# The output matrix's transposing jobs, two at a time between pieces of the first batch's key and query products

## The chip, the cores and the metric
One core of a Trainium2 chip runs the whole program. The metric is the device time in microseconds from start to end; three runs of the kernel before gave 2906.24, 2908.05 and 2908.42 us. TensorE multiplies and turns tiles into PSUM, VectorE, ScalarE and GpSimd work on them, and SyncE issues the transfers. Each engine takes its own list of instructions in order and waits on counting semaphores for the others.

## What is computed
The reference is a small tower over 64 batches of 128 rows and 1024 columns:

```python
h = _L0_tok_ref(log_dt, x, B, inv_A_real, A_imag, 1024)   # state-space kernel over 1024 steps
h = h + _L0_attn_ref(_layernorm(h), wq, wk, wv, wo)       # 32 heads, 8 for keys and values, rotation, causal softmax
h = h + _L0_ffn_ref(_layernorm(h), W_base, b_base, lora_A, lora_B, router_W, router_b, prior, active)
```

The attention's mask leaves every causal position in for 128 rows. The last step is a dense layer with four low-rank experts, mixed by a router.

## The kernel before
A first stage (`token_kernel`, to about 215 us) makes the rows `h` and stores them. A second (`tower`) goes through the batches, one turn for each: a turn for `b` does attention for batch `b`, the key, value and query products for `n = b + 1`, the first norm for `m = b + 2`, the output product for `b - 1` and the dense layer for `b - 2`. The turns for `b = -2` and `b = -1` have only the parts that exist: the norm of batch 0, then the products of batch 0 and the norm of batch 1. Every engine has its own version of `turn`, and the order of work is what is written there, with counting semaphores between the engines.

All products are in 16 bit with split operands: a weight is kept as a high and a low half, so a dense product is, for each of eight pieces of 128 rows of the weight, three matmuls of 512 columns (`dense`). `kv(c0, c1)` does pieces c0 to c1 of the key and value product into a bank, `q(0, ...)` and `q(1, ...)` those of the two halves of the query product; each of the three has 24 matmuls.

The weights come as 32 bit and have to be turned and divided. That is a list of 56 jobs (`jobs`): 0 to 23 for query, key and value (`J_O` = 24), 24 to 39 for the output matrix (`J_B` = 40), 40 to 55 for the base matrix of the dense layer; `MID` is 30. A job is three steps on three engines: TensorE turns a part into a PSUM bank (`turn`; 4 transposes, for the output matrix 16 matmuls by the identity, on 32 columns each), ScalarE writes the high half from the bank (`high`), VectorE the low half (`low`), which counts `s_wlo`. The banks go round: a job waits until the low half of the job that had its bank before is done (`before`). `spread(i)` is one small matmul that gives the maximum over all partitions of a matrix to every partition; from it come the scales (`powers`).

What stands around the change, in the order of each engine:

- TensorE: jobs 10 to 29, `spread(4)`, then the turn for `b = -1`: `kv`, `q(0)`, `q(1)`, and `pe_close` with jobs 30 to 39. The turn for `b = 0` begins with the first score product, which waits for low half 38 (and the second for 39), then `spread(2)`, two jobs of the base matrix, and the key product of batch 1.
- ScalarE: `act_after` does the high halves of jobs 14 to 29, then waits for scale 4 and copies `lbs` (the low-rank experts' matrix). Then comes the turn for `b = -1`: sums of absolute values of the base matrix's eight parts (`base_sums`, for its scale), the 16-bit copies of the rotated heads (`heads_high`: k, 0, 1, 2, 3), the value half, the two instructions of the norm, and the high halves 30 to 39, at places that `act_early` gives by a name (`0`, `2`, `"norm"`, `"last"`).
- VectorE: `after` does the low halves 10 to 23, the maximum of `lbs` and its column for `spread(4)`, the low halves 24 to 29, the scale from `spread(4)`, and the low part of `lbs`. Then the turn for `b = -1`: the rotations of keys and queries (`rope`), the low parts of the heads, the statistics of the norm, and the low halves 30 to 39 by `early`.
- GpSimd adds the two parts of a rotation, and does the two small operations and the low half of the norm.
- SyncE issues the transposing transfers of heads and of normed rows, each behind the low part that it needs.

`after` and `act_after` stand ahead of the turn for `b = -1` on their engines. PSUM banks 2 and 3 hold `lbs` until its low part is done; job 32 waits for that.

Of the kernel before, what the change touches and what calls it, by code (L numbers as in the profile page):

```python
# [28 lines left out]
NQ, NO = NQKV // P, D // P  # L29
# [564 lines left out]
def prepare_weights(nc, sem, w, keep, ring, ps_b, ps_ar):  # L594
# [80 lines left out]
    class Prep:  # L675
        wlo, wt, lbs, bias, ps = s_wlo, s_wt, s_lbs, s_bias, s_ps
        ar_made, ar_copied, base_row = s_ar, s_arraw, s_rows[2]
        done_a, done_c, done_score, done_pv, done_half = last_a + 1, last_c + 1, (last[0] + 1, last[1] + 1), last[4] + 1, last[3] + 1
        jb, jend, mid = J_B, J_END, MID

# [71 lines left out]
        @staticmethod  # L752
        def act_early(act, b, k, unused):
            def base_sums(i0, i1):
                for i in range(i0, i1):
                    act.wait_ge(s_wb[GROUP[i]], 16 * GROUP.count(GROUP[i]))
                    if i:
                        act.wait_ge(s_sums, i)
                    nc.scalar.activation(unused, raw_a[:, NQ - NO + i], ACT.Abs,
                                         accum_out=part_max[:, i:i + 1]).then_inc(s_sums, 1)  # L760

            if b == -1 and k == 0:
                base_sums(0, 4)
            if b == -1 and k == 2:
                base_sums(4, 6)
            if b == -1 and k == "norm":
                Prep.high(act, MID, MID + 4)
                base_sums(6, NO)
            if b == -1 and k == "last":
                Prep.high(act, MID + 4, J_B)  # L770
            if b == 0 and k != "norm" and k != "last":
                Prep.high(act, J_B + 2 * k, J_B + 2 * k + 2)

        @staticmethod
        def dve_tools(dve):
# [97 lines left out]

            def early(b, k):
                if b == -1 and k == "last":
                    low(MID, MID + 4)
                    dve.wait_ge(s_sums, NO)
                    V.tensor_reduce(mx[:, 2:3], part_max[:, 0:NO], AX_X, ALU.max).then_inc(s_mx, 1)
                    columns(2)
                if b == -1 and k == "end":  # L880
                    low(MID + 4, J_B)
                if b == 0 and k == 0:
# [61 lines left out]
        def pe_open(pe, rows):  # L944
# [19 lines left out]
            ins.then_inc(s_ps, 1)  # L964
            Prep.turn(pe, 10, MID)
            Prep.spread(pe, 4)

        @staticmethod
        def pe_close(pe):

            Prep.turn(pe, MID, J_B)

# [3 lines left out]
def tower(nc, sem, tok_h, keep, w, ring_of, token_programs, out):  # L976
# [5 lines left out]
    with ExitStack() as ctx:  # L982
# [353 lines left out]
        def _(act):  # L1336
# [3 lines left out]
            def turn(b, par, attention, qkv, norm, rest, finish):  # L1340
# [74 lines left out]
                if qkv:  # L1415
                    act.wait_ge(s_kv, n + 1)

                    if rest and some(p):
                        act.wait_ge(s_pv, p * 2 + 2)
                    A(v_hi[:, 1 - par], bank_a[1][:, HKV * HD:2 * HKV * HD], ACT.Copy, scale=LSHIFT).then_inc(s_vhi, 1)  # L1420
                if attention:
                    probs_high(b, 1)
# [55 lines left out]
        def _(dve):  # L1478
# [10 lines left out]
            def turn(b, par, attention, qkv, norm, rest, finish):  # L1489
# [149 lines left out]
                if qkv:  # L1639
                    v_low()  # L1640
                if norm:
                    dve.wait_ge(s_hin, m * 16 + 16)
                    half_stats(hin, 0, stats1, s_bn1)
                    half_stats(hin, 1, stats1, s_bn1)
                    spread(stats1, mv1, mean1, var1, marks[:, 2:3], s_bn1, s_rstd1, m)
# [25 lines left out]
                if finish:  # L1671
# [14 lines left out]
                    zb = za[:, :].unsqueeze(1).to_broadcast([P, 2, NA * R])  # L1686
                    TT(zs[:, 1], zb, zs[:, 0], ALU.subtract).then_inc(s_zs, 1)
                if qkv:
                    rope(2)
# [33 lines left out]
        def _(pe):  # L1723
# [3 lines left out]
            def turn(b, par, attention, qkv, norm, rest, finish):  # L1727
# [116 lines left out]


                if attention:
                    scores(0)
# [21 lines left out]
                if qkv:  # L1869
                    q(1, 5, 8)  # L1870
                if qkv and not attention:
                    prep.pe_close(pe)
                if closing:
# [124 lines left out]
```

## Time and profile before
| | us |
|---|---|
| median of three runs | 2908.05 |
| lowest, highest | 2906.24, 2908.42 |
| the profiled execution | 2908.48 |
| its span, first to last instruction | 2906.8 |

| engine | busy us | share of the span |
|---|---|---|
| TensorE matmuls | 2802.0 | 96% |
| VectorE | 2370.6 | 82% |
| GpSimd | 1972.0 | 68% |
| ScalarE | 1919.0 | 66% |

Times in a trace count from the first instruction of the profiled execution. An instruction's line is that of kernel.py; where a helper issues many, all of them have the helper's line: 1782 is `dense`, 920 and 924 are `turn`, 941 is `spread`, 721 is `high`, 826 is `low`, 759 is `base_sums`. Two f32 passes make one matmul by the identity, so a job of the output matrix shows as 32 instructions. A timeline merges like instructions that follow each other: start, time to the last one's end, count. Several matmuls overlap, so their pace is read from their starts.

### The profile page before, as it was taken

What the parts mean: (1) busy time and instruction counts of PE and PEld (TensorE: products, weight loads), DVE (VectorE), ACT (ScalarE), POOL (GpSimd) and SP (SyncE); (2) the same over time, 40 slices, a digit from 0 to 9 for tenths busy, and PEclk for the clock granted to TensorE, in tenths of its full rate; (3) what the DMA queues carried; (4) which work ended last, traced back from release to release, by engine and by line L of the source; (5) the groups of instructions that cost most, each with busy time, mean ns of one, the idle gap of its engine ahead of it and who ended that gap; (6) DMA issues with size and microseconds to landing.
All of it is one profiled execution on the core that took longest, in us unless ns stands there. A gap on an engine that the chain in (4) does not pass through costs nothing.

```text
span 2906.8 us, 61868 instructions
## 1 busy us (share of the span) xinstructions
PE 2802.0 (96%) x16932; PEld 1410.0 (49%) x16932; DVE 2370.6 (82%) x8774; ACT 1919.0 (66%) x5987; POOL 1972.0 (68%) x1731
## 2 busy tenths in 40 slices
PE   6788899999999999999999999999999999999987
PEld 5665444444444444444444444444444444444433
DVE  9987788888888888888888888888888888888774
ACT  8987666666666666666666666666666666666652
POOL 4532677777777777777777777677776777777762
PEclk8999899999999999999999999999999999999989
DMA  7884676666666666666666666666666666666662
GB/s 244 235 217 134 139 154 146 153 149 148 153 147 150 150 149 149 151 149 149 152 149 145 151 149 153 150 144 152 148 155 149 145 150 147 156 145 152 142 131 62
DMA packets 1220851, 442.64 MB, mean 152 GB/s; under 512 B 1167120, under 2 KB 1175568, under 8 KB 1220640
## 3 DMA queue, kind: packets, MB, share of 16 engines
q1 hardware_dynamic: 1220640, 440.69, 66.4%
q14 instruction: 183, 1.50, 0.2%
q8 instruction: 28, 0.46, 0.1%
HBM read 88.22 MB, written 67.11 MB: 53 GB/s over the span
## 4 chain that ended last, share of the span: by engine, by line
PE 89%; DVE 4%; issue 2%; ACT 2%; DMA 1%; POOL 1%; SPq 0%; DVEq 0%; ACTq 0%; POOLq 0%
PE bank_b L1782 45%; PE bank_a L1782 22%; PE bank_c L1782 11%; PE score L1745 4%; PE kps L581 2%; PE pv L1771 2%; PE bank_b L1771 1%; DVE z L507 1%; DVE z L506 1%; PE pv L1884 1%; DMA xc<-in_x_dram 1%; ACT probs L1352 0%; PE pv L1842 0%; PE bank_c L1842 0%; DVE u L477 0%
## 5 line engine op out<-in xcount | busy, mean ns | idle before, releaser
L1352 ACT ACTIVATE probs<-probs,negmax 128x128 f32<-128x128 f32 x2048 | 789.6, 387 | 254.6 <-DVE negmax L1503 254.5
L1265 POOL TENSOR_TENSOR p_hl<-probs,p_hl 128x512 f16<-128x512 f32 x512 | 618.1, 1207 | 342.4 <-ACT p_hl L1361 339.8
L1261 POOL TENSOR_TENSOR probs<-probs,rsum 128x512 f32<-128x512 f32 x512 | 556.7, 1088 | 191.0 <-DVE rsum L1514 190.7
L1503 DVE CUSTOM_DVE_ANT_0 probs<-score,table,scal 128x128 f32<-128x128 f32 x2048 | 598.6, 347 | 81.3 <-issue 80.9
L1782 PE MATMUL bank_a<-qkv_hi,xt 128*128 128x512 f16 x2048 | 641.5, 380 | 2.0 <-DMA xt<-xy_hl 2.0
L1782 PE MATMUL bank_b<-b_hi,yt 128*128 128x512 f16 x2016 | 631.8, 380 | 0.0
L1361 ACT ACTIVATE p_hl<-probs 128x512 f16<-128x512 f32 x512 | 320.0, 625 | 433.4 <-POOL probs L1261 433.4
L1557 DVE TENSOR_TENSOR heads<-rope_a,heads 128x512 f16<-128x512 f32 x320 | 391.7, 1240 | 30.0 <-ACT heads L1382 29.9
L1782 PE MATMUL bank_b<-o_hi,at_hi 128*128 128x512 f16 x1024 | 389.3, 380 | 1.5 <-ACT at_hi L1367 1.5
L1782 PE MATMUL bank_b<-o_lo,at_hi 128*128 128x512 f16 x1024 | 389.3, 380 | 0.0
L1782 PE MATMUL bank_b<-o_hi,at_lo 128*128 128x512 f16 x1024 | 389.1, 380 | 0.0
L1782 PE MATMUL bank_a<-qkv_lo,xt 128*128 128x512 f16 x1024 | 388.9, 380 | 0.0
L1782 PE MATMUL bank_b<-b_lo,yt 128*128 128x512 f16 x1008 | 383.0, 380 | 0.0
L1352 ACT ACTIVATION_READ_ACCUMULATOR probs<-probs,negmax 128x1 f32 x2048 | 382.2, 187 | 0.0
L1782 PE MATMUL bank_c<-qkv_hi,xt 128*128 128x512 f16 x1024 | 325.9, 380 | 0.0
L1782 PEld LDWEIGHTS bank_a<-qkv_hi,xt 128*128 128x128 f16 x2048 | 200.8, 98 | 222.3 <-DMA xt<-xy_hl 2.2
L1782 PEld LDWEIGHTS bank_b<-b_hi,yt 128*128 128x128 f16 x2016 | 197.3, 98 | 217.0 <-issue 1.9
L1280 POOL TENSOR_TENSOR xy_hl<-xyn,xy_hl 128x1024 f16<-128x1024 f32 x128 | 272.7, 2131 | 31.1 <-ACT xyn L1396 26.1
L1382 ACT ACTIVATE heads<-rope_a 128x512 f16<-128x512 f32 x320 | 192.5, 620 | 91.5 <-POOL rope_a L1271 86.2
L1271 POOL TENSOR_TENSOR rope_a<-rope_a,rope_b 128x512 f32<-128x512 f32 (+1 forms) x192 | 208.7, 1087 | 40.5 <-DVE rope_b L1540 37.7
L1745 PEld LDWEIGHTS score<-kstack,stack 128*128 128x128 f16 x2048 | 155.0, 98 | 119.9 <-issue 7.2
L1274 POOL TENSOR_TENSOR rstd<-var,minus_half 128x1 f32<-128x1 f32 x128 | 70.9, 554 | 206.1 <-DVE var L1569 205.7
(226 smaller groups left out, 4580.0 us busy)
## 6 DMA issues: line engine op xcount, KB each, us to landing
hin<-tok_h SPq DMA_DIRECT2D x64, 512.0 KB, 3.3
r<-tok_h SPq DMA_DIRECT2D x64, 512.0 KB, 3.8
out_dram<-r SPq DMA_DIRECT2D x63, 512.0 KB, 2.9
tok_h<-kout SPq DMA_DIRECT2D x60, 512.0 KB, 6.1
probs_t<-p_hl SPq DMA_TRANSPOSE x512, 3.1
xc<-in_x_dram SPq DMA_DIRECT2D x32, 128.0 KB, 4.2
raw_a<-in_L_attn_wq_dram SPq DMA_DIRECT2D x4, 1024.0 KB, 9.5
raw_b<-in_L_attn_wo_dram SPq DMA_DIRECT2D x8, 512.0 KB, 4.6
```

The lines of the kernel that those rows point to most:

```text
L1261: TT(x, x, rsum[:, u % 4].unsqueeze(2).to_broadcast([P, GR, T]), ALU.mult).then_inc(s_norm, 1)
L1265: TT(p_hl[:, u % 2, 1], probs[:, u % 4], p_hl[:, u % 2, 0], ALU.subtract).then_inc(s_plo, 1)
L1271: TT(rope_a[:, 0:hs], rope_a[:, 0:hs], rope_b[:, 0:hs], ALU.add).then_inc(s_rope2, 1)
L1280: TT(xy_hl[:, 1], xyn[:, :], xy_hl[:, 0], ALU.subtract).then_inc(done, 1)
L1352: ins = A(probs[:, u % 4, g], probs[:, u % 4, g], ACT.Exp, bias=negmax[:, u % 4, g:g + 1], scale=-1.0, accum_out=sums[:, u % 4, g:g + 1])
L1361: A(p_hl[:, u % 2, 0], probs[:, u % 4], ACT.Copy).then_inc(s_phi, 1)
L1382: A(dst, src, ACT.Copy).then_inc(s_hhi, 1)
L1503: ins = V.tensor_tensor_reduce(probs[:, u % 4, g], score[u % 2][:, g], mask, col(U_SC), 3e38, ALU.add, ALU.min, negmax[:, u % 4, g:g + 1])
L1557: TT(dst, full_.unsqueeze(2).to_broadcast([P, 8, 2, HD]), hi, ALU.subtract).then_inc(s_hlo, 1)
L1745: ins = MM(score[u % 2][:, g], stack[:, h // 8, h % 8], kstack[:, par, u], start=True, stop=True)
L1771: ins = MM(half_out[a][32 * k:32 * k + 32].rearrange("p g t -> p (g t)"), v[:, 1 - par, (4 * a + k) * HD:(4 * a + k + 1) * HD], probs_t[:, ...
L1782: ins = MM(bank, x(c), w[:, c, cols], start=(c == 0 and i == 0), stop=(c == KC - 1 and i == 2))
```

## The change
TensorE no longer does jobs 24 to 29 and `spread(4)` ahead of the turn for `b = -1`, nor jobs 30 to 39 behind it. In that turn it waits for low half 23 and then does pieces of the products with two jobs between them. The highs and lows of jobs 30 to 39 go to more places of the same turn on ScalarE and VectorE, under the new names `"v"` and `"rope"`, and the sums of the base matrix are divided otherwise. `after` and `act_after` are as they were.

```diff
             if b == -1 and k == 0:
-                base_sums(0, 4)
+                base_sums(0, 2)
             if b == -1 and k == 2:
-                base_sums(4, 6)
+                Prep.high(act, MID, MID + 2)
+                base_sums(2, 4)
+            if b == -1 and k == "v":
+                Prep.high(act, MID + 2, MID + 4)
+            if b == -1 and k == 3:
+                Prep.high(act, MID + 4, MID + 6)
             if b == -1 and k == "norm":
-                Prep.high(act, MID, MID + 4)
-                base_sums(6, NO)
+                base_sums(4, 7)
             if b == -1 and k == "last":
-                Prep.high(act, MID + 4, J_B)
+                Prep.high(act, MID + 6, J_B)
+                base_sums(7, NO)
...
             def early(b, k):
+                if b == -1 and k == 0:
+                    low(MID, MID + 2)
+                if b == -1 and k == "v":
+                    low(MID + 2, MID + 4)
+                if b == -1 and k == "rope":
+                    low(MID + 4, MID + 6)
                 if b == -1 and k == "last":
-                    low(MID, MID + 4)
+                    low(MID + 6, MID + 8)
+                if b == -1 and k == "end":
+                    low(MID + 8, J_B)
                     dve.wait_ge(s_sums, NO)
                     V.tensor_reduce(mx[:, 2:3], part_max[:, 0:NO], AX_X, ALU.max).then_inc(s_mx, 1)
                     columns(2)
-                if b == -1 and k == "end":
-                    low(MID + 4, J_B)
...
-            Prep.turn(pe, 10, MID)
-            Prep.spread(pe, 4)
-
-        @staticmethod
-        def pe_close(pe):
-
-            Prep.turn(pe, MID, J_B)
+            Prep.turn(pe, 10, J_O)
...
+                if qkv and not attention:
+                    def o_jobs(j0, j1):
+                        prep.turn(pe, prep.jo + j0, prep.jo + j1)
+
+                    pe.wait_ge(prep.wlo, prep.jo)
+                    kv(0, 2)
+                    o_jobs(0, 2)
+                    kv(2, 4)
+                    prep.spread(pe, 4)
+                    o_jobs(2, 4)
+                    kv(4, 6)
+                    o_jobs(4, 6)
+                    kv(6, 8)
+                    q(0, 0, 3)
+                    o_jobs(6, 8)
+                    q(0, 3, 6)
+                    o_jobs(8, 10)
+                    q(0, 6, 8)
+                    q(1, 0, 3)
+                    o_jobs(10, 12)
+                    q(1, 3, 6)
+                    o_jobs(12, 14)
+                    q(1, 6, 8)
+                    o_jobs(14, 16)
+                    return
```

In ScalarE's turn `"v"` stands behind the value half and ahead of the head copies 0 and 1; the head copy 2 stands between `"norm"` and `"last"`. In VectorE's turn `"v"` stands behind the low part of the values and ahead of the statistics, `"rope"` ahead of the last rotation; the low part of heads 2 stands between `"last"` and `"end"`.

## Rows read from the trace of the kernel before
**Rows 1.** The page, busy tenths in 40 equal slices of the span.
```profile
PE   6788899999999999999999999999999999999987
```
**Rows 2.** Table by stretch, one regular batch turn; columns as in its second line.
```profile
core 0: us, PE busy (x) PEld busy (x) DVE busy (x) ACT busy (x) POOL busy (x), PEclk, DMA share, GB/s
424.00:467.50 43.50, 43.50 (x261) 20.87 (x260) 35.34 (x146) 27.90 (x95) 30.90 (x29) 1.00 0.67 149
```
**Rows 3.** Order of time, TensorE, 229 to 264 us: start, us, what, [idle before].
```profile
229.24 3.70 PE L920 MATMUL wt<-const,raw_b 128*32 128x128 f32 x128
...
235.19 0.49 PE L941 MATMUL wt<-const,wide 128*128 128x128 f32 x2
235.51 0.38 PE L1782 MATMUL bank_a<-qkv_hi,xt 128*128 128x512 f16 x1
...
250.84 0.38 PE L1782 MATMUL bank_c<-qkv_hi,xt 128*128 128x512 f16 x1
251.15 7.37 PE L920 MATMUL wt<-const,raw_b 128*32 128x128 f32 x256
...
262.69 0.38 PE L1745 MATMUL score<-kstack,stack 128*128 128x128 f16 x4 [0.80 <-DVE o_lo L826]
...
263.19 1.04 PE L924 MATMUL wt<-const,raw_a 128*128 128x128 f32 x8
```
**Rows 4.** Order of time, VectorE, 223 to 264 us.
```profile
223.62 7.42 DVE L826 SCALAR_TENSOR_TENSOR qkv_lo<-wt,scal,qkv_hi 128x512 f16<-128x512 f32 x10 [1.28 <-ACT qkv_hi L721]
...
238.92 2.58 DVE L870 SCALAR_TENSOR_TENSOR lbs<-ps_b,scal,lbs 32x1024 f16<-32x1024 f32 x2 [1.18 <-ACT lbs L749]
...
241.66 0.42 DVE L1537 TENSOR_TENSOR rope_a<-bank_a,table 128x256 f32<-128x256 f32 x1
...
247.67 1.28 DVE L1560 BATCH_NORM_STATS2 stats<-hin 128x6 f32<-128x512 f32 x2
...
258.11 0.29 DVE L797 TENSOR_SCALAR wide<-const,mx 128x128 f32<-128x128 f32 x1
...
259.04 4.38 DVE L826 SCALAR_TENSOR_TENSOR o_lo<-wt,scal,o_hi 128x512 f16<-128x512 f32 x6
```
**Rows 5.** Order of time, ScalarE, 237 to 261 us.
```profile
237.77 1.11 ACT L749 ACTIVATE lbs<-ps_b,scal 128x1024 f16<-128x1024 f32 x1 [1.77 <-DVE scal L866]
238.78 1.05 ACT L759 ACTIVATE probs<-raw_a 128x1024 f32<-128x1024 f32 x1
...
240.01 1.06 ACT L759 ACTIVATE probs<-raw_a 128x1024 f32<-128x1024 f32 x1
...
248.81 1.15 ACT L1382 ACTIVATE heads<-rope_a 128x512 f16<-128x512 f32 x2 [2.09 <-POOL rope_a L1271]
250.88 1.24 ACT L1435 ACTIVATE xy_hl<-hin,shift,rstd 128x1024 f16<-128x1024 f32 x1 [0.92 <-POOL shift L1276]
...
258.31 2.40 ACT L721 ACTIVATE o_hi<-wt,scal 128x512 f16<-128x512 f32 x4
```
**Rows 6.** Order of time, GpSimd, the keys' rotation.
```profile
242.57 0.73 POOL L1271 TENSOR_TENSOR rope_a<-rope_a,rope_b 128x256 f32<-128x256 f32 x1 [17.34 <-DVE rope_b L1540]
```
**Rows 7.** Everything on the turned rows xt, 215 to 270 us: issues (ns) and landings.
```profile
L1223 SPq DMA_TRANSPOSE xt<-xy_hl x2: 1760/2118/2477, 225.3 to 255.5; - x2
...
DMA to landing us min/median/max: 3.8/4.9/6.0
```
**Rows 8.** Table by stretch, columns as in rows 2: the granted clock around idle stretches.
```profile
217.20:220.40 3.20, 0.00 (x0) 0.00 (x0) 2.40 (x8) 2.59 (x4) 0.56 (x1) 1.00 0.04 17
222.00:228.60 6.60, 5.94 (x28) 5.54 (x28) 5.11 (x8) 5.84 (x9) 2.13 (x1) 0.50 0.68 169
262.60:280.00 17.40, 17.31 (x104) 9.88 (x105) 13.45 (x53) 12.10 (x38) 5.53 (x6) 1.00 0.14 32
300.00:304.00 4.00, 1.93 (x10) 1.58 (x11) 2.84 (x13) 3.05 (x9) 2.19 (x2) 0.50 0.65 135
304.00:308.00 4.00, 4.00 (x13) 1.46 (x11) 2.00 (x8) 2.50 (x10) 0.27 (x1) 0.60 0.70 155
```
**Rows 9.** Who waited for whom, TensorE, 262 to 304 us: us, times, longest.
```profile
PE wt L924 <- DVE b_lo L826: 12.1, 4, 3.9
```

More of the change, by code:

```diff
@@ L678, in prepare_weights @@
         done_a, done_c, done_score, done_pv, done_half = last_a + 1, last_c + 1, (last[0] + 1, last[1] + 1), last[4] + 1, last[3] + 1
-        jb, jend, mid = J_B, J_END, MID
+        jo, jb, jend = J_O, J_B, J_END
         @staticmethod
@@ L762, in act_early @@
             if b == -1 and k == 0:
-                base_sums(0, 4)
+                base_sums(0, 2)
             if b == -1 and k == 2:
-                base_sums(4, 6)
+                Prep.high(act, MID, MID + 2)
[4 more added lines that the diff above has]
+                Prep.high(act, MID + 4, MID + 6)
             if b == -1 and k == "norm":
-                Prep.high(act, MID, MID + 4)
-                base_sums(6, NO)
+                base_sums(4, 7)
             if b == -1 and k == "last":
-                Prep.high(act, MID + 4, J_B)
-            if b == 0 and k != "norm" and k != "last":
+                Prep.high(act, MID + 6, J_B)
+                base_sums(7, NO)
+            if b == 0 and isinstance(k, int):
                 Prep.high(act, J_B + 2 * k, J_B + 2 * k + 2)
@@ L1420, in turn @@
                     A(v_hi[:, 1 - par], bank_a[1][:, HKV * HD:2 * HKV * HD], ACT.Copy, scale=LSHIFT).then_inc(s_vhi, 1)
+                early("v")
                 if attention:
@@ L1640, in turn @@
                     v_low()
+                early("v")
                 if norm:
@@ L1687, in turn @@
                     TT(zs[:, 1], zb, zs[:, 0], ALU.subtract).then_inc(s_zs, 1)
+                early("rope")
                 if qkv:
@@ L1870, in turn @@
                     q(1, 5, 8)
-                if qkv and not attention:
-                    prep.pe_close(pe)
                 if closing:
```

## The prediction
> **What bounds the kernel now.** I read the page first for the share of TensorE by slice [rows 1]: 90% or more from the sixth slice almost to the end. A table by stretch then gives one batch turn of the regular ones [rows 2]: TensorE is busy for all of its 43.5 us, at a granted clock of 1.00. So from about 350 us on TensorE alone sets the time, and whatever the change does can count only as a shift of the moment at which that regime is reached. The change touches the stretch from 229 to 263 us, the tail of the preparation; there I read the order of time of TensorE [rows 3], VectorE [rows 4], ScalarE [rows 5] and GpSimd [rows 6].
>
> What the reader is to see there: before, TensorE does jobs 24 to 29 from 229.24, the key and query products from 235.51 to 251.05, jobs 30 to 39 from 251.15, and reaches the first score product at 262.69, with a wait of 0.80 us for job 38's low half. It is never far from done, and neither is anybody else: ScalarE's last high half of the stretch ends only just ahead, by 262.7 (its low half is the last of six that end at 263.42 [rows 4]). The stretch has two near-critical engines, TensorE with some 31 us of work and ScalarE, and the second keeps up only because it starts its share of the stretch (the `lbs` copy, then sums, copies and halves) at 237.77 [rows 5].
>
> **The change part by part.** Jobs are numbered in the list: 24 to 39 are the output matrix's, a high half (ScalarE) and a low half (VectorE) belong to each.
>
> *The products start earlier.* In the new order they stand behind job 23 and wait for the 24th low half. Those of the last ten jobs of the query, key and value weights run on VectorE from 223.62 for 7.42 us [rows 4], so to 231.04; the turned rows, issued at 225.3, land 3.8 to 6.0 us later [rows 7], at 231.3 at the latest, which would add no more than 0.2. TensorE is done with job 23 when it starts job 24 before, at 229.24, and waits 1.9 us. The products begin at 231.1 instead of 235.51.
>
> *Jobs 24 to 29 come later.* A product matmul costs 0.216 us (235.51 to 250.84 are 71 of them [rows 3]), a job 0.925 (four in 3.70 from 229.24), the spread matmul 0.3 (235.19 to 235.51). From the last product at 250.84 to the first job at 251.15 pass 0.31, so a change to a job costs 0.1 over the matmul's own time. Jobs 24 to 29 are three groups of six matmuls and two jobs: 3 x (1.30 + 0.10 + 1.85) + 0.3 = 10.0 us; job 29 ends at 241.1, where before it ended at about 235.2, when the spread matmul started.
> The Trainium skill says ("TensorE: Matmul & The Clock Gate", Part 2, Step-by-step) that the next tile's weights are loaded while the present matmul runs. By that a change of operand would be free, and the sum below would be 0.3 us smaller; the row at 251.15 shows 0.1 each time, and the row decides.
>
> *Who waits for job 29.* This is the price of the change. `after()` and `act_after()` are not touched: VectorE still does the low halves of jobs 24 to 29 before it makes scale 4, and ScalarE the high halves before it copies `lbs`; only behind these stand the rotation of the keys, the sums and everything else of the turn. Before, ScalarE's `lbs` began at 237.77, 2.6 us behind job 29's end, VectorE's `lbs` at 238.92 for 2.58 and the first rotation at 241.66 [rows 4, 5]. With job 29 at 241.1 each of them comes 6.0 us later: `lbs` 243.8 on ScalarE and 245.0 on VectorE, first rotation 247.6. In the meantime ScalarE and VectorE idle between the pairs of jobs. The early halves of the products bring nothing, because their consumer, the rotation, stands behind that queue.
>
> *ScalarE's account from `lbs` to the last high half.* Work: `lbs` 1.0; seven sums at 1.24 (238.78 to 240.01 is one; the eighth stands behind) 8.7; four head copies at 0.53 (a pair from 248.81 [rows 5]) 2.1; the value half, of half a head copy's size, 0.3; the normalising pair, two of 1.24 that overlap by a tenth, 2.3; ten high halves at 0.6 (four in 2.40 from 258.31 [rows 5]) 6.0. Together 20.4. Waits: the key copy needs GpSimd's add of the rotation, before at 242.57 for 0.73 [rows 6], now 248.6 to 249.4, while ScalarE is through with `lbs` and two sums at 247.3: 2.1. The next head copies wait about 0.2. The normalising pair needs the statistics on VectorE and two small operations of GpSimd behind them: before, it began at 250.88, 3.2 us behind the statistics' start at 247.67 [rows 4, 5]. VectorE now comes to them only behind the low half of job 33, at about 256, so the pair can begin at 259.1, and ScalarE is through with job 35 at 257.6: 1.5. So 20.4 + 3.8 = 24.2, and the last high half ends at 268.1; before it ended by 262.7. None of the late start is made up: before, the same stretch took 24.9 us with one sum more.
> What is last in it: the copy of query heads 2 stands behind the sums 4 to 6, and the high halves of jobs 36 to 39 behind that copy. The first of them starts at 265.65.
>
> *VectorE and the first score product.* Low halves 36 and 37 (0.67 each, six in 4.38 from 259.04 with waits [rows 4]), the low part of heads 2 (0.6), low half 38 (0.74): from 266.4 to 269.1. The score product waits for exactly this, 269.1 against 262.69: **+6.4**. TensorE by its own sum would have been through with job 39 at 262.7 (241.1, then 54 matmuls at 0.216, five changes at 0.1, ten jobs at 0.925, 11.7 + 0.5 + 9.3 = 21.5), so it stands idle for 6.4 us.
> Behind the first score stands the spread of the base maxima. Before, its column was made at 258.11 [rows 4] and hid entirely; now the reduction over eight numbers and the column (0.29) stand behind low half 39: 269.7 + 0.5 = 270.2. TensorE waits another 0.8, and the first job of the base matrix starts at 270.4 against 263.19: **+7.2**.
>
> *The clock.* Between 217.2 and 220.4 TensorE did nothing; from 222.0 to 228.6 the granted clock was 0.50, the lower level of 1.2 GHz, so low for 6.6 us at least. From 300 to 304 TensorE had worked 1.9 us of 4, the last 1.9 of them, at 0.50; from 304 to 308 it was busy throughout at a mean of 0.60, so low for 3.2 us and then at 1.00: 5.1 us of dense work at the lower level [rows 8]. After 6.4 idle us the new restart at 270 should be the same. At half rate 5.1 us of dense work cost 2.5 us, 6.6 us cost 3.3, none cost 0. I take **+2.5**, from the second case, where the waits before it were of the like length and the pieces are the same (score, key product). It lies on the path: from 262.6 to 280 TensorE is busy for 17.31 of 17.40 us before [rows 8], and each score product releases the next step of the softmax.
>
> *What costs nothing.* Dividing the sums and halves into other portions changes no instruction's length. The loads of the base matrix wait for jobs up to 23, which don't move. SyncE's queue moves with its releasers: heads k, then heads 0 and 1, the next rows, the turned rows for batch 1. These are issued behind GpSimd's low half at about 263.7 and land 6.0 us later at worst [rows 7], 269.7, and the key product wants them at 271.3: covered by 1.6 us; if that cover goes, each us beyond it is a us.
>
> *The sum.* Against the profiled execution of 2908.48 us (span 2906.8): +7.2 + 2.5 = +9.7, so 2918.2; the median of the three runs lies 0.43 below that execution, so 2917.8 us. Does the shift pass on? After 283 us TensorE waits for low halves of base jobs, 12.1 us in four waits of at most 3.9 [rows 9]. These waits belong to a chain maxima, exponentials, high half, low half, next score, which starts with the first score products; it moves as a whole. I therefore let nothing be absorbed.
>
> **The rivals.**
> *TensorE sets the end (not slower).* Place: 231 to 262. If the high and low halves kept within one job of TensorE, the score product would follow job 39 as before. TensorE's own sum ends at 262.7, or 261.1 without the changes' 0.1; the wait of 0.80 us vanishes, one of 1.9 comes. Price between -2.1 (if the 1.9 us were not waited either) and +0.8: 2906 to 2909. It decides at the first high half of job 36: that must start on ScalarE by about 260. Against it: it stands behind a copy that needs the second query product, which ends at 261.
> *ScalarE makes up its idle time.* If the three waits of 3.8 us in its account close (statistics earlier, key copy not late), the score comes at 265.3, and the idle time of TensorE is short enough that I charge half of the clock's price: +3.4 + 1.2, with some of the waits left +5: 2911 to 2913.9.
> *Slack behind swallows the clock's loss.* The 12.1 us of waits after 283 hide TensorE's slowness, only the shift of the halves remains: +7.2, 2915; with some of the shift hidden too, 2914. For it: in these waits VectorE and ScalarE are the bound. Against: until 280 TensorE runs without a wait and gives out the scores.
> *The clock costs more.* It stays low for 6.6 us (3.3), and the wait of 1.9 us at 229, right after a low stretch, lowers it once more, so that the first pieces up to job 29 run at half rate and delay `lbs` by 1.7 to 3: 2920 to 2924.
>
> **How the numbers follow.** Forecast (2916 to 2920) 0.55; clock's loss swallowed (2913.9 to 2916) 0.15; ScalarE makes up (2911 to 2913.9) 0.10; clock costs more 0.12; TensorE sets the end 0.06; something that gains over 0.2%, for which I find no term, 0.02. A measurement of this kernel can tell about 0.2%, 5.8 us, from no change. Slower than 2913.9: 0.55 + 0.15 + 0.12 = 0.82, of which I move 0.02 to the middle because two of the cases end at that bound; within 0.2%: 0.06 + 0.10 + 0.02 = 0.18; faster 0.02. The range from 2911 to 2922 leaves out the not slower case and about half of the dear clock.
>
> **What would show it.** First product at 231.1 behind a wait for a low half of the qkv weights; `lbs` on ScalarE near 243.8; first rotation near 247.6; the high half of job 36 near 265.6 behind the copy of heads 2; a TensorE wait of about 6 us for an output-matrix low half ahead of the first score, near 269; granted clock 0.5 behind that. I am wrong if ScalarE's `lbs` comes before 241, if the first score comes before 265, or if the batch turns at 400 us lie less than 5 us later than before.

## The result, and the profile after

The changed kernel takes 2917.33 us (median of 8 runs, 2914.99 to 2920.73) against 2908.2 us (8 runs of the kernel before, 2906.24 to 2909.47): a ratio of 1.0032, interval 1.0022 to 1.0043; the medians differ by 9.1 us. Its profiled execution took 2918.61 us with a span of 2917.0, so 10.1 us more in time and 10.2 in span than the one before. The forecast was 2917.8, from 2911 to 2922, with "slower" at 0.80.

The regular turn is what it was. On the page, PE's slices are at nine tenths from the sixth almost to the end as in [rows 1]; in the table by stretch (columns as in [rows 2]) the same stretch has no idle TensorE and a granted clock of 1.00. The other four lines are of the changed stage.
```profile
424.00:467.50 43.50, 43.50 (x260) 20.73 (x258) 35.17 (x145) 27.78 (x91) 31.48 (x28) 1.00 0.71 152
231.00:234.00 3.00, 1.44 (x10) 1.20 (x8) 2.79 (x5) 2.14 (x4) 0.00 (x0) 0.89 1.11 268
270.00:274.00 4.00, 1.85 (x10) 1.62 (x11) 3.96 (x16) 3.69 (x7) 0.00 (x0) 0.50 0.55 125
274.00:278.00 4.00, 4.00 (x18) 2.30 (x17) 2.60 (x8) 2.62 (x10) 0.00 (x0) 0.75 0.38 70
276.00:280.00 4.00, 4.00 (x20) 1.79 (x19) 1.41 (x2) 0.62 (x2) 0.00 (x0) 1.00 0.25 40
```
The changed stage, TensorE in order of time (to be read against [rows 3]):
```profile
234.25 0.39 PE L1790 MATMUL bank_a<-qkv_hi,xt 128*128 128x512 f16 x1 [1.80 <-DVE qkv_lo L831]
...
235.33 0.38 PE L1790 MATMUL bank_a<-qkv_hi,xt 128*128 128x512 f16 x1
235.64 1.96 PE L931 MATMUL wt<-const,raw_b 128*32 128x128 f32 x64
237.53 0.39 PE L1790 MATMUL bank_a<-qkv_hi,xt 128*128 128x512 f16 x1
...
244.32 0.39 PE L1790 MATMUL bank_a<-qkv_hi,xt 128*128 128x512 f16 x1
...
264.04 1.95 PE L931 MATMUL wt<-const,raw_b 128*32 128x128 f32 x64
271.77 0.59 PE L1753 MATMUL score<-kstack,stack 128*128 128x128 f16 x4 [5.78 <-DVE o_lo L831]
272.73 0.80 PE L952 MATMUL wt<-const,wide 128*128 128x128 f32 x2 [0.37 <-DVE wide L802]
273.32 1.92 PE L935 MATMUL wt<-const,raw_a 128*128 128x128 f32 x8
...
280.06 0.39 PE L1753 MATMUL score<-kstack,stack 128*128 128x128 f16 x4
```
TensorE is through with job 39 at 266.0 and then stands idle for 5.78 us: the first score product waits for a low half of the output matrix. ScalarE shows why (against [rows 5]):
```profile
236.85 1.50 ACT L721 ACTIVATE o_hi<-wt,scal 128x512 f16<-128x512 f32 x2 [3.54 <-PE wt L931]
240.30 0.69 ACT L721 ACTIVATE o_hi<-wt,scal 128x512 f16<-128x512 f32 x1 [1.95 <-PE wt L931]
...
246.91 1.11 ACT L749 ACTIVATE lbs<-ps_b,scal 128x1024 f16<-128x1024 f32 x1 [1.77 <-DVE scal L871]
...
252.46 0.63 ACT L1387 ACTIVATE heads<-rope_a 128x512 f16<-128x512 f32 x1 [2.16 <-POOL rope_a L1276]
...
261.85 1.24 ACT L1441 ACTIVATE xy_hl<-hin,shift,rstd 128x1024 f16<-128x1024 f32 x1 [0.96 <-POOL shift L1281]
...
267.72 0.63 ACT L1387 ACTIVATE heads<-rope_a 128x512 f16<-128x512 f32 x1
268.26 2.40 ACT L721 ACTIVATE o_hi<-wt,scal 128x512 f16<-128x512 f32 x4
```
It idles 3.54 and 1.95 us ahead of the halves of the spread-out jobs, comes to `lbs` at 246.91, and the last four high halves (jobs 36 to 39) stand at 268.26 behind the copy of query heads 2. VectorE follows it (against [rows 4]):
```profile
226.88 7.31 DVE L831 SCALAR_TENSOR_TENSOR qkv_lo<-wt,scal,qkv_hi 128x512 f16<-128x512 f32 x10 [1.28 <-ACT qkv_hi L721]
...
250.81 0.42 DVE L1543 TENSOR_TENSOR rope_a<-bank_a,table 128x256 f32<-128x256 f32 x1
...
268.96 1.41 DVE L831 SCALAR_TENSOR_TENSOR o_lo<-wt,scal,o_hi 128x512 f16<-128x512 f32 x2 [3.45 <-ACT o_hi L721]
...
272.39 0.29 DVE L802 TENSOR_SCALAR wide<-const,mx 128x128 f32<-128x128 f32 x1
```

**Three pieces of the difference.** The first of these lines ends at 234.19; the row of before for the same ten halves ends at 231.04 [rows 4]. Up to that end (call it E24, the 24th low half) the two kernels do the same work, yet it came 3.15 us later. So the difference of the two spans has three pieces: up to E24, from E24 to the first job of the base matrix (BJ, the row of eight matmuls on `raw_a`), and from BJ to the span's end. One pair of executions doesn't tell which of these belongs to the kernel. The table has further executions of both kernels, and of the experiments below; all in us, each from one profile. "Second score" is the next score product behind BJ.

| kernel | E24 | `lbs` on ScalarE after E24 | first score after E24 | BJ after E24 | BJ to second score | BJ to the end | span |
|---|---|---|---|---|---|---|---|
| before | 231.04 | 6.73 | 31.65 | 32.15 | 5.40 | 2643.6 | 2906.8 |
| before, second execution | 232.22 | 6.73 | 31.65 | 32.14 | 5.41 | 2641.9 | 2906.3 |
| before, third execution | 229.57 | 6.74 | 31.65 | 32.15 | 5.41 | 2641.7 | 2903.4 |
| changed | 234.19 | 12.72 | 37.58 | 39.13 | 6.74 | 2643.7 | 2917.0 |
| changed, timed again | 229.93 | 14.35 | 39.20 | 40.75 | 7.74 | 2645.5 | 2916.2 |
| changed, third execution | 231.12 | 12.73 | 37.60 | 39.14 | 7.30 | 2644.5 | 2914.8 |
| changed, fourth execution | 230.88 | 12.74 | 37.59 | 39.13 | 6.63 | 2643.4 | 2913.4 |
| first six undone | 234.76 | 6.73 | 34.96 | 36.51 | 6.53 | 2643.2 | 2914.5 |
| last ten undone | 230.38 | 14.35 | 38.55 | 39.05 | 5.41 | 2643.4 | 2912.8 |
| halves ahead of sums | 233.90 | 12.74 | 33.44 | 38.80 | 7.80 | 2645.6 | 2918.3 |
| queues mended | 232.00 | 12.72 | 33.73 | 35.01 | 9.96 | 2647.7 | 2914.7 |
| TensorE kept busy | 232.87 | 12.74 | 37.60 | 38.88 | 5.40 | 2644.0 | 2915.7 |
| before, reordered | 230.57 | 6.73 | 30.20 | 30.70 | 5.40 | 2641.8 | 2903.1 |

Means over the three executions of before and the four of the changed kernel: span 2905.5 and 2915.35, so +9.85, of which +0.6 lies up to E24 (230.94 to 231.53), **+7.4** from E24 to BJ (32.15 to 39.54) and **+1.9** behind BJ (2642.4 to 2644.3). This is the table on which the rest of the text rests. The executions come from several chips, so small differences of whole times between its rows prove little.

### The profile page after: what moved, and what is told of

Its sections match the earlier page's. It is cut to its first block, busy times and chain, and to the rows that moved or that the text cites. A ratio compares the mean times of both kernels' runs of the same rounds, so it can differ in the third digit from the quotient of the medians.

```text
span 2917.0 us, 61869 instructions
## 1 busy us (share of the span) xinstructions
PE 2806.1 (96%) x16932; PEld 1410.5 (48%) x16932; DVE 2365.4 (81%) x8774; ACT 1919.9 (66%) x5987; POOL 1970.4 (68%) x1731
## 4 chain that ended last, share of the span: by engine, by line
PE 89%; DVE 3%; ACT 2%; DMA 2%; issue 2%; POOL 1%; SPq 1%; DVEq 0%; ACTq 0%; POOLq 0%
PE bank_b L1790 45%; PE bank_a L1790 22%; PE bank_c L1790 11%; PE score L1753 4%; PE kps L581 2%; PE pv L1779 2%; PE bank_b L1779 1%; DMA tok_h<-kout 1%; DMA xc<-in_x_dram 1%; PE pv L1916 1%; ACT probs L1357 1%; PE pv L1850 0%; PE bank_c L1850 0%; ACT kout L358 0%; DVE probs L1509 0%
```

## The experiments

Two theories were to be told apart. *The queues*: the price is made by the order in which ScalarE and VectorE take their work, since `lbs`, and with it the rotations and sums, stands behind the halves of jobs 24 to 29. *The clock*: most of it is TensorE at its lower level after idle time, and the shift of the queues is hidden in part. A third, raised by the 3.15 us above, is that the first stage of the changed kernel is itself slower. Each ratio below is to the kernel before as timed beside that run: 2907.68 us for halves ahead of sums, queues mended, and before reordered, 2906.40 for the other four.

**Both kernels once more.** No edit; the kernels of before and after, unchanged.

> The kernel before unaltered, one more profile. In question is the end of the 24th low half, up to which both kernels issue the same work: 231.0 in the first profile of before, 234.2 and 229.9 in the two of the changed kernel. Theory (the clock of TensorE falls at different places of the first stage in each execution): anywhere from 229.5 to 235, and 32.2 us from there to the first base-matrix job as before. Rival (the kernel before has a shorter first stage): within 0.5 us of 231.0 again.

> The same once more. Theory: the 24th low half anywhere from 229.5 to 235, not tied to the other look. Rival: within 0.5 us of 231.0.

> The changed kernel unaltered, a third profile. Theory: the 24th low half anywhere from 229.5 to 235; from there to the first base-matrix job 39.0 to 40.8 us, the longer one where the first products run at the lower clock; scores 1 another 6.7 to 7.8 behind it. Rival (its first stage is longer): 233 or later.

> The same once more, with the same numbers for each theory; with it four profiles of the changed kernel say how often the first products run at the lower clock.

The single times are 2907.90 and 2905.04 us for before, 2916.43 and 2915.03 for the changed kernel. E24 is 232.22 and 229.57 for before, 231.12 and 230.88 for the changed kernel: these four show nothing of the 3.15 us. BJ stands 32.15 behind E24 in all three executions of before to within 0.01, and 39.13 in three of four of the changed kernel. So +6.98 is the price of the stage in those three, and it repeats far better than the whole time does; the fourth is the next run.

**The changed kernel, timed again.** No edit.

> The changed kernel unaltered, on the same chip as the next three, and a second profile of it. Theory (the tail of the preparation costs 7 us, the clock behind it 1 to 2, and the rest of the 10.2 us between the two first profiles is the clock in the first stage, which drops at places that differ from one execution to the next): about +9 us against the kernel before, 1.0031; in this profile the difference of the first base-matrix job to the end of the 24th low half stays at 39.1 us (32.2 before), while the 24th low half itself may lie anywhere from 230 to 235 us. Rival (the change slows the first stage too, by the 3.1 us seen): the 24th low half lies again at 234 or later.

2917.82 us, ratio 1.0036 (1.0022 to 1.005). E24 lies at 229.93, so the rival of a slower first stage (234 or later) does not come. BJ was expected 39.1 behind E24 and stands at 40.75. Its trace has one thing that the other three lack: `lbs` comes 14.35 us behind E24 and not 12.72, and with it everything up to BJ 1.6 later. The reason is on TensorE, in order of time and in the table by stretch:
```profile
229.99 0.39 PE L1790 MATMUL bank_a<-qkv_hi,xt 128*128 128x512 f16 x1 [1.98 <-DVE qkv_lo L831]
...
231.68 3.27 PE L931 MATMUL wt<-const,raw_b 128*32 128x128 f32 x64
```
```profile
225.00:231.00 6.00, 3.93 (x25) 2.33 (x24) 6.00 (x9) 3.71 (x6) 0.00 (x0) 1.00 0.95 266
231.00:234.00 3.00, 3.00 (x47) 2.16 (x48) 0.35 (x2) 0.25 (x1) 0.00 (x0) 0.51 1.03 410
```
Behind the wait of 1.98 us for the 24th low half the granted clock falls from 1.00 to 0.51, and jobs 24 and 25 take 3.27 us instead of 1.96. That is the mechanism that the prediction named as a rival (the dear clock). It happened in two of the eight profiles that have this wait (here and with the last ten undone), and not in the one of the result, where jobs 24 and 25 take 1.96 us.

**Only the last ten jobs spread.** The first six stand ahead of the products again.
```
-            Prep.turn(pe, 10, J_O)
+            Prep.turn(pe, 10, MID)
+            Prep.spread(pe, 4)
...
-                    pe.wait_ge(prep.wlo, prep.jo)
-                    kv(0, 2)
-                    o_jobs(0, 2)
...
-                    kv(6, 8)
+                    kv(0, 8)
```


> The changed kernel with one part undone: jobs 24 to 29 and the spread stand ahead of the products again; jobs 30 to 39 stay between pieces of the query product. Theory (two chains lead to the late end: the late start of lbs, and the late end of the second query product, which ends at 259 here and at 251 before): lbs starts at its old place, 6.7 us behind the 24th low half; the first base-matrix job comes +4.2 us against the kernel before instead of +7.2, with the clock about +5 to +6 in all, 2913 to 2914. Rival (only the late start of lbs costs): the score comes within 1 us of the kernel before, 2908 to 2909. Rival (only the spreading of jobs 30 to 39 costs): no better than the changed kernel, 2917.

2914.45 us, ratio 1.0026 (1.0015 to 1.0037). `lbs` is back at 6.73 behind E24, exactly as before, so it is the first six jobs that delay it; yet BJ is still 4.36 later than before (4.2 expected). ScalarE and TensorE:
```profile
241.49 1.11 ACT L749 ACTIVATE lbs<-ps_b,scal 128x1024 f16<-128x1024 f32 x1 [1.77 <-DVE scal L871]
...
256.51 1.15 ACT L1388 ACTIVATE heads<-rope_a 128x512 f16<-128x512 f32 x2 [3.43 <-POOL rope_a L1277]
```
```profile
269.72 0.38 PE L1754 MATMUL score<-kstack,stack 128*128 128x128 f16 x4 [4.94 <-DVE o_lo L831]
```
The query products now end later, because jobs stand between them, so the copy of query heads 0 and 1 waits 3.43 us for the rotation (before, 2.09 for two copies [rows 5]); what stands behind it is late, and TensorE waits 4.94 for a low half. The time was missed: 2913 to 2914 was expected, 5 to 6 us above before, and it is 8.05 above. The distances give 5.5 at the second score; E24 of this execution is 234.76, the latest in the table, and why is not shown.

**Only the first six spread.** The last ten stand behind the products again, with halves and sums in the order of before.
```
-                    q(0, 0, 3)
-                    o_jobs(6, 8)
...
-                    q(1, 6, 8)
-                    o_jobs(14, 16)
+                    q(0, 0, 8)
+                    q(1, 0, 8)
+                    o_jobs(6, 16)
```


> The other part undone: jobs 24 to 29 stay between pieces of the key product, jobs 30 to 39 stand behind the query products with their halves and the sums in the old places. Theory (the late lbs alone makes ScalarE late, whatever follows): lbs 12.8 us behind the 24th low half as in the changed kernel, 6.0 later than before; the first base-matrix job +6.0 us, TensorE without a wait of more than 3 us there so that the clock costs little: 2914 to 2915. Rival (the spreading of jobs 30 to 39 is the cause): within 1 to 2 us of the kernel before, 2909 to 2910.

2912.72 us, ratio 1.0022 (1.0013 to 1.0031), so 6.3 us above before. BJ +6.90 (6.0 expected). In this execution jobs 24 and 25 take 3.00 us behind the first wait and `lbs` stands at 14.35; if these 1.6 us pass on to BJ whole, as they do in the changed kernel timed again, 5.3 are left. Here no TensorE idle time of 5 us is left ahead of the score:
```profile
232.41 3.00 PE L920 MATMUL wt<-const,raw_b 128*32 128x128 f32 x64
...
261.02 7.12 PE L920 MATMUL wt<-const,raw_b 128*32 128x128 f32 x192 [3.42 <-DVE o_lo L826]
268.93 0.38 PE L1742 MATMUL score<-kstack,stack 128*128 128x128 f16 x4 [0.80 <-DVE o_lo L826]
```
The wait has moved ahead of jobs 34 to 39, which need the banks that the low halves set free. The clock stays up (1.00 from 266 to 278), and BJ to the second score is 5.41 as before. Up to BJ the last ten jobs alone cost 4.4 us and the first six alone 5.3, both together 7.0: the two do not add. Both make ScalarE's work late, the first six by `lbs`, the last ten by the rotation of the queries.

**The last high halves ahead of the sums.** In the changed kernel, ScalarE does jobs 36 to 39 at "norm", ahead of sums 4 to 6, and VectorE's four low halves move to "last".
```
             if b == -1 and k == "norm":
+                Prep.high(act, MID + 6, J_B)
                 base_sums(4, 7)
             if b == -1 and k == "last":
-                Prep.high(act, MID + 6, J_B)
                 base_sums(7, NO)
```


> The changed kernel with another order on ScalarE and VectorE alone: the high and low halves of jobs 36 to 39 stand ahead of sums 4 to 7 and of the copy of query heads 2. Theory (ScalarE's whole work is late, and its order only chooses which of its consumers waits): the first score comes 4 to 5 us earlier, 33.5 us behind the 24th low half instead of 37.6, but the spread of the base maxima, whose last sums now stand behind, waits so much longer; the first base-matrix job stays within 0.5 us of 39.1 behind the 24th low half, and the time that of the changed kernel within 1 us. Rival (the place of four halves behind the copy is the cause): the whole 4 us come back, about 5 us above the kernel before.

2917.21 us, ratio 1.0032 (1.002 to 1.0044).
```profile
267.34 0.38 PE L1752 MATMUL score<-kstack,stack 128*128 128x128 f16 x4 [1.63 <-DVE o_lo L831]
272.11 0.80 PE L951 MATMUL wt<-const,wide 128*128 128x128 f32 x2 [4.39 <-DVE wide L802]
272.70 1.91 PE L934 MATMUL wt<-const,raw_a 128*128 128x128 f32 x8
```
The score comes 4.1 us earlier (33.44 behind E24), but the spread matmul behind it then waits 4.39 us for the column, which needs all eight sums. BJ gains 0.33 and the time nothing. Here the order only chooses which of two waits stands last; the work ahead of both is the same and began late.

**The queues mended.** In the changed kernel, sums 0 to 2 go into ScalarE's idle time between the spread-out jobs, the others move up, and the halves of jobs 36 to 39 come ahead of the copy of heads 2, on VectorE ahead of its low part.
```
         def act_after(act, unused):
-            Prep.high(act, 14, MID)
+            Prep.high(act, 14, J_O + 2)
+            Prep.base_sums(act, unused, 0, 1)
+            Prep.high(act, J_O + 2, J_O + 4)
+            Prep.base_sums(act, unused, 1, 2)
+            Prep.high(act, J_O + 4, MID)
+            Prep.base_sums(act, unused, 2, 3)
...
             if b == -1 and k == "norm":
-                base_sums(4, 7)
-            if b == -1 and k == "last":
-                Prep.high(act, MID + 6, J_B)
+                Prep.high(act, MID + 6, MID + 8)
                 base_sums(7, NO)
+                Prep.high(act, MID + 8, J_B)
```


> The changed kernel's order on TensorE, with ScalarE's late work mended: three of the base sums fill its waits between the pairs of jobs ahead of lbs, and the last four halves stand ahead of the copy of heads 2, the sums' maximum ahead of its low part. Theory (ScalarE's late start is most of the price, and TensorE's own order gains nothing): the first base-matrix job comes about 4 us later than in the kernel before, measured from the 24th low half (36.4 us behind it, 32.2 before, 39.1 changed), the time 4 to 6 us above the kernel before. Rival (TensorE's order, the wait of 1.9 us and the eight changes, is the price): no better than the changed kernel. Rival (only ScalarE): equal to the kernel before.

2916.25 us, ratio 1.0028 (1.0017 to 1.004). BJ is 35.01 behind E24, 4.1 earlier than in the changed kernel: the queue theory's step came, and by more than expected (36.4). So the order of the queues makes 4.1 of the 7.0 us. The 2.9 that are left are not all of one kind: TensorE is through with job 39 at 31.8 behind E24, here as in the changed kernel, and at 30.85 before, so its new order, with its first wait and its changes, costs 1.0 there; the score's wait is 1.1 longer than before, and between score and BJ pass 0.8 more, with a wait of 0.57 for the column. The time did not follow: 8.6 us above before, where 4 to 6 were expected. TensorE, then its clock by stretch, then SyncE's issue of the turned rows:
```profile
265.73 0.38 PE L1759 MATMUL score<-kstack,stack 128*128 128x128 f16 x4 [1.92 <-DVE o_lo L839]
...
267.01 1.79 PE L941 MATMUL wt<-const,raw_a 128*128 128x128 f32 x8
270.97 0.61 PE L1796 MATMUL bank_a<-qkv_hi,xt 128*128 128x512 f16 x1 [2.18 <-DMA xt<-xy_hl]
...
276.97 0.39 PE L1759 MATMUL score<-kstack,stack 128*128 128x128 f16 x4
```
```profile
266.00:270.00 4.00, 2.22 (x12) 1.71 (x10) 3.70 (x19) 3.59 (x12) 0.00 (x0) 0.64 1.44 169
270.00:274.00 4.00, 3.03 (x8) 1.10 (x9) 1.41 (x2) 1.17 (x3) 0.00 (x0) 0.51 0.45 99
```
```profile
264.29 2.53 SPq L1234 DMA_TRANSPOSE xt<-xy_hl  x1
```
The key product of batch 1 comes for its rows at 268.8 (267.01 + 1.79); they land 6.6 us behind their issue, and it starts at 270.97: this is the cover that the prediction costed at nothing and gave 1.6 us. In the changed kernel the rows were issued at the same distance from E24 (32.29), landed 5.2 us later and so 3.3 us ahead of the product; with TensorE 4 us earlier and a landing of 6.6 us the cover is gone. The wait of 2.18 us and the clock of 0.64 and 0.51 around it make BJ to the second score 9.96 us instead of 5.40 before, and the way from BJ to the end is the longest in the table.

**TensorE kept busy.** Behind job 39 the changed kernel gets 24 matmuls whose result nothing reads.
```
                     o_jobs(14, 16)
+                    for _ in range(24):
+                        MM(router, keep["qkv_hi"][:, 0, 0:P], keep["qkv_hi"][:, 0, 0:512], start=True, stop=True)
```


> The changed kernel with 24 matmuls more (5.2 us of work at the higher clock) on TensorE behind job 39, into a bank that nothing reads; they fill the idle time ahead of the first score. It prices the clock alone. Theory (the idle time lowers the clock and the restart runs at half rate): the granted clock stays at 1.00 behind the first score, scores 1 come 5.9 us behind the first base-matrix job's release as before instead of 6.7 to 8.3, and the whole is 1 to 2 us faster than the changed kernel. Rival (the loss is swallowed behind): the same as the changed kernel within 0.5 us though the clock is up. Rival (the first score waits for the extra matmuls): slower.

2915.28 us, ratio 1.0028 (1.0017 to 1.004).
```profile
270.47 0.38 PE L1753 MATMUL score<-kstack,stack 128*128 128x128 f16 x4 [0.49 <-DVE o_lo L831]
271.42 0.49 PE L952 MATMUL wt<-const,wide 128*128 128x128 f32 x2 [0.57 <-DVE wide L802]
271.75 1.04 PE L935 MATMUL wt<-const,raw_a 128*128 128x128 f32 x8
...
277.15 0.39 PE L1753 MATMUL score<-kstack,stack 128*128 128x128 f16 x4
```
```profile
270.00:274.00 4.00, 2.96 (x21) 2.10 (x22) 3.83 (x19) 3.70 (x12) 0.00 (x0) 1.00 0.33 74
```
The score comes 37.60 behind E24, as in the changed kernel, so the idle time is a result of the queues and not a cause. The clock from 270 to 274 is 1.00 and not 0.50; BJ comes 0.25 earlier than in the changed kernel, and BJ to the second score is 5.40, the value of before. That shows, in one execution, that the 1.2 to 2.3 us lost there in the changed kernel are the clock's. Whether they reach the end is less sure: the median is 2.5 us below that of the changed kernel in the same comparison (2917.82), but the intervals overlap, and from BJ to the end this execution took 2644.0, inside the range of the changed kernel's four.

**The kernel before, reordered.** The opposite test: the sums 6 and 7 go into a wait of ScalarE in the kernel before, its high halves 30 to 35 come at "norm", and VectorE does low halves 34 and 35 with them.
```
+            if b == -1 and k == "v":
+                base_sums(6, NO)
             if b == -1 and k == "norm":
-                Prep.high(act, MID, MID + 4)
-                base_sums(6, NO)
+                Prep.high(act, MID, MID + 6)
             if b == -1 and k == "last":
-                Prep.high(act, MID + 4, J_B)
+                Prep.high(act, MID + 6, J_B)
```
(VectorE's low halves in the same portions. A second edit puts the low halves of jobs 10 and 11 ahead of the first norm's statistics; what it brings would lie ahead of E24, at 230.57 here, and can't be told from E24's wandering.)

> The kernel before, not the changed one, with what the study points to: jobs stay where they were, two base sums move into ScalarE's wait for the rotated queries, so that the halves of jobs 34 to 39 come sooner, and the low halves of jobs 10 and 11 stand ahead of the first norm's statistics on VectorE. Theory (the stretch is bound by ScalarE's queue, and TensorE's waits of 1.4 us for job 38 and 3.3 us for job 14 are its mark): 1.5 us from the sums and up to 1 us from the low halves, 0.9991 to 0.9995, about the limit of what these rounds can tell. Rival (other waits take their place): equal to the kernel before.

2905.72 us, ratio 0.9994 (0.9985 to 1.0003) to the kernel before.
```profile
250.67 8.94 PE L921 MATMUL wt<-const,raw_b 128*32 128x128 f32 x320
260.77 0.38 PE L1747 MATMUL score<-kstack,stack 128*128 128x128 f16 x4 [1.16 <-DVE o_lo L827]
```
Jobs 30 to 39 now run in one piece of 8.94 us, and BJ comes 30.70 behind E24, 1.45 earlier than before. The trace shows the gain at its place; the time, 2.0 us lower with an interval that holds 1, doesn't prove an improvement. The trace does show how little there is to win on TensorE in this stage: of the time from job 24 to the score TensorE waits 1.5 us here (0.37 for job 28 and 1.16 for the score).

## Why the prediction was right, step by step

The chain that the prediction names is the one that the traces show; of its two terms, the stage (+7.2) is close and the clock (+2.5) is mis-sized. The marks are compared as distances from E24, which the prediction had at 231.04.

- *Products start behind a 1.9-us wait for a qkv low half*: 1.80, at the place named. Three pieces of six products and two jobs: job 29's successor starts at 244.32, 10.1 behind E24, and the prediction had 10.06. A change from products to a job takes 0.31 from start to start (235.33 to 235.64), 0.1 over a product's 0.216, as taken from [rows 3]. The Trainium skill's view that weights load while the present matmul runs ("TensorE: Matmul & The Clock Gate", Part 2, Step-by-step) does not make this change free here.
- *`lbs` on ScalarE and the first rotation*: 12.72 measured and 12.8 predicted; 16.62 and 16.56. That `lbs` stands behind jobs 24 to 29 and not behind the products is shown by the run with the first six undone, where it returns to 6.73.
- *ScalarE's account*: the key copy waits 2.16 (2.1 predicted), the head copies 0.64 (0.2), the normalising pair 0.96 (1.5). The high half of job 36 starts 34.07 behind E24 (34.6), behind the copy of heads 2, as said; none of the late start was made up.
- *First score*: 37.58 behind E24 (38.06), so +5.9 and not +6.4: ScalarE took 21.35 us from `lbs` to the high half of job 36 (21.85), with the same 3.8 us of waits, so 0.5 less work than charged. TensorE idled 5.78 (6.4).
- *The spread*: +0.37 of waiting for the column, not +0.8; but at the lower clock its own work and the score's take longer, and BJ comes 39.13 behind E24 (39.36). The stage's sum of +7.2 came to +6.98.
- *The clock, +2.5*: the term that was mis-sized. The clock is at 0.50 from 270 to 274 and at 0.75 from 274 to 278, and back at 1.00 from 276: with the first score at 271.77 that is 4.2 us at the lower level, not 5.1. Of it 1.5 us lie ahead of BJ, beside the column's wait; the run with TensorE kept busy has BJ 0.25 earlier, so that much of the clock's price is in the +6.98 already. Behind BJ the loss was 1.34, 2.34, 1.90 and 1.23 us in four executions (6.74, 7.74, 7.30 and 6.63 less 5.40), a mean of 1.7. Over the whole way from BJ to the end it is 1.9 in the means; with 1.9 us of spread among three executions of before, that agreement is rough. The case that the 2.5 was taken from is not as like as the prediction says: it has four waits of at most 3.9 us with work between them [rows 9], where here one lasts 5.78.
- *Nothing is absorbed behind*: true, and to within 0.02 us. The score products of batch 0 are eight; the ninth stands behind the four waits for base jobs [rows 9]. It is the first of these lines before, and the second in the changed kernel:
```profile
302.95 0.63 PE L1745 MATMUL score<-kstack,stack 128*128 128x128 f16 x4
```
```profile
314.41 0.64 PE L1753 MATMUL score<-kstack,stack 128*128 128x128 f16 x4
```
  From the second score (268.59, which is BJ at 263.19 and the table's 5.40, and 280.06) that is 34.36 and 34.35 us, and it is 34.35 to 34.37 in all thirteen executions.
- *The turned rows are covered*: true in the changed kernel, where the key product at 275.03 waits for nothing; and shown to be a thin cover by the mended queues.
- *The rivals*: TensorE did not set the end (it idled 5.78 us), ScalarE did not make up its idle time, the slack did not swallow the clock's loss, as the ninth score shows. The dear clock is real, but belongs to some executions: +1.6 on `lbs` in two of eight. The prediction put its condition at "right after a low stretch"; the traces say otherwise, as the last section shows.

Forecast and result agree to 0.5 us of 2917, and this is closer than the working deserves. The profiled pair differs by 10.2, of which 3.15 arose up to E24, where the programs are the same, 6.98 in the stage, and about nothing behind BJ (2643.6 and 2643.7, though the executions of before differ by 1.9 among themselves in that part). Only the means over several executions show the predicted parts, +7.4 and +1.9, and 0.4 of the 7.4 is the dear clock of a single execution. At the second score the four executions of the changed kernel lie 8.3, 10.9, 8.9 and 8.2 us behind before (45.87, 48.49, 46.44 and 45.76 against 37.55), where the prediction has 9.7; their mean is 9.1, which is also the difference of the medians. Three of the four lie 0.8 to 1.5 us under the prediction and one 1.2 over, by a clock event that its sum left out; that the median comes within 0.5 us of the forecast is in part luck.

The range of E24 over all profiles, 229.6 to 234.8, is half of the effect; what makes it is not settled. It goes roughly with the clock of the first stage: E24 is 229.6 to 230.6 in the four profiles whose mean granted clock from 100 to 231 us is 0.96 or 0.97, and 230.9 to 234.8 in the nine with 0.93 to 0.95. The place of the low stretch differs too. One row, of the kernel before and then of the changed one, TensorE in order of time:
```profile
124.52 3.71 PE L581 MATMUL kps<-v,z 128*128 128x256 f32 x16 [2.75 <-POOL z L275]
```
```profile
125.07 5.40 PE L581 MATMUL kps<-v,z 128*128 128x256 f32 x16 [2.58 <-POOL z L275]
```
The same sixteen matmuls took 3.71 and 5.40 us; from 120 to 130 the mean clock was 1.00 before and 0.83 after. From 130 to 140 it is the other way round, 0.83 and 1.00. Whether the changed program makes E24 later at all was not shown: it is 229.6 to 232.2 in four profiles of programs with the old order, 229.9 to 234.8 in nine with the new one or a part of it.

## What to carry to other kernels

When work is moved on one engine, look at what stands in program order behind its *consumers* on the other engines: here TensorE had the same work in another order, which costs it about 1 us, and most of the +7 us came from `lbs`, rotations and sums that came late in ScalarE's and VectorE's queues; 4.1 us of it went when these queues were put in another order. In the two runs on that, moving late halves ahead in the queue only chose which wait was last, and putting work into idle time brought 4.1 us up to BJ, whereupon a transfer that had been covered came late. Measure a change in an early stage by distances from a mark that the change can't reach: the stage's repeat to 0.01 us in most executions here, while the mark itself wanders over 5.

## What the runs showed of the hardware

Behind a wait of 1.8 to 2.0 us on TensorE the granted clock falls in some executions and not in others, and the level ahead of it goes the other way from what the prediction had supposed. The table by stretch has the six microseconds up to 231 of the changed kernel's first profile, at 0.50, which is the lower level of 1.2 GHz:
```profile
225.00:231.00 6.00, 5.28 (x25) 4.88 (x25) 4.62 (x7) 5.40 (x9) 2.13 (x1) 0.50 0.51 145
```
The wait of 1.80 us ends at 234.25; the clock was up by then, 0.89 from 231 to 234, and stayed up, 1.00 from 234 to 237. Five further profiles with this wait have 0.54 to 0.89 from 225 to 231 and 1.00 from 231 to 237. The two in which the clock fell, to 0.51 and 0.53 from 231 to 234, have 1.00 from 225 to 231. So in all eight, the clock fell behind this wait exactly where it had been high from 225 on; in the other six it was low for at least a part of that stretch and rose ahead of the wait's end. Eight profiles show that this goes together, and no run was made to show why. The Trainium skill says that the moment of a change varies because the hardware's watch does not start anew with a kernel ("TensorE: Matmul & The Clock Gate", Part 1, What's actually happening); that the same wait does not always have the same effect agrees with it, and no run here shows the watch itself.

After the idle 5.78 us the clock was low in all four executions of the changed kernel, for 2.5 to 4.7 us behind BJ (an estimate: twice the loss there, at half rate).

One transposing transfer took 6.6 us to land in the run with mended queues, where those of before took 3.8 to 6.0 [rows 7]: the longest landing in one trace is no bound for another.
